# Two sets of buffers for the first layer norm, and the query rotation moved into the loop over head pairs

## The reference

```python
# x: (8, 4096, 1024) float32; _layernorm has no weights, eps 1e-5
x = x + attn_a(_layernorm(x))   # linear attention: elu(Q)+1, elu(K)+1, KV = K^T V, context = Q KV / Z, @ Wo.T + bo
x = x + ffn(_layernorm(x))      # gelu(x @ w1 + b1) @ w2 + b2, 1024 -> 4096 -> 1024
x = x + attn_b(_layernorm(x))   # below
x = x + ffn(_layernorm(x))

# attn_b: 16 heads of 64; causal softmax attention
q = (x @ Wq) split in heads
k = low-rank keys: x @ Wk (192 columns), expanded by key_decoder
v = low-rank values: x @ Wv (192 columns), expanded by value_decoder
q = _apply_rope(q, cos, sin)
k = _apply_rope(k, cos, sin)
attn = softmax(mask(q k^T / 8))
y = (attn v) @ Wproj
```

## Time and profile before

| | us |
|---|---|
| median of two runs of the kernel | 6642.1 (6566.71 and 6717.48) |
| the profiled execution, its own time | 6563.59 |
| its span on the slowest core (core 0) | 6562.1 |
| spans of the other cores | 6528.1 to 6555.6 |

### The profile page before, as it was taken

The page is one execution under the profiler, slowest core; times in us unless marked ns, Lnnn a source line. Parts: engine busy times, 40 slices in busy tenths (PEclk is TensorE's granted clock), DMA queues, the critical chain, the costliest instruction groups (busy, mean ns, idle before and its releaser), DMA issues.

```text
span 6562.1 us, 55992 instructions; the slowest of 8 cores (6528.1 to 6562.1 us)
## 1 busy us (share of the span) xinstructions
PE 4754.6 (72%) x19134; PEld 1766.6 (27%) x19408; DVE 1540.7 (23%) x2479; ACT 1823.9 (28%) x2415; POOL 81.6 (1%) x158
## 2 busy tenths in 40 slices
PE   2299767775996888572877777777785556996777
PEld 0033222222442333221222222222221112442333
DVE  3344354451001222127022022012102440000000
ACT  1110011102331000000755855765672002330000
POOL 0000000000001000000000000000000000001000
PEclk6599888887998888795877877977887777998888
DMA  2200211114226333200000000000003224226333
GB/s 65 64 1 1 39 52 52 39 39 101 76 76 146 103 103 103 63 0 0 6 5 5 6 6 5 6 6 5 5 6 97 84 91 96 75 76 146 109 103 115
DMA packets 258100, 356.21 MB, mean 54 GB/s; under 512 B 19173, under 2 KB 166885, under 8 KB 255526
## 3 DMA queue, kind: packets, MB, share of 16 engines
q1 hardware_dynamic: 236294, 304.50, 14.1%
q0 software_dynamic: 21536, 48.12, 4.2%
HBM read 257.93 MB, written 142.74 MB: 61 GB/s over the span
## 4 chain that ended last, share of the span: by engine, by line
PE 61%; DVE 12%; ACT 11%; DMA 8%; issue 5%; DVEq 2%; POOL 1%; ACTq 1%; SPq 0%; POOLq 0%
ACT expb L833 7%; PE f2pyo L569 7%; PE f1pyo L569 7%; PE f1pph L523 6%; PE f2pph L523 6%; PE py L797 4%; PE psc L814 4%; PE py L801 3%; PE pr L917 2%; PE ppt L475 2%; PE ppk L303 2%; PE ppb L457 2%; PE p L668 2%; PE pkv L341 2%; PE ppv L311 2%
## 5 line engine op out<-in xcount | busy, mean ns | idle before, releaser
L833 ACT ACTIVATE expb<-psc 128x1024 bf16<-128x1024 f32 x896 | 892.6, 1023 | 179.7 <-PE psc L821 167.5
L797 PE MATMUL py<-expb,vpair 128*65 128x512 bf16 (+3 forms) x1152 | 469.3, 407 | 297.5 <-ACT expb L833 275.3
L569 PE MATMUL f2pyo<-f2hb,f2w 128*128 128x512 bf16 x2007 | 467.2, 394 | 153.8 <-DMA f2hb<-scr_h 123.8
L523 PE MATMUL f1pph<-xnt,f1w 128*128 128x512 bf16 x2007 | 446.7, 381 | 63.6 <-DMA f1w<-w 57.4
L523 PE MATMUL f2pph<-xnt,f2w 128*128 128x512 bf16 x2007 | 445.8, 380 | 62.6 <-DMA f2w<-w 56.4
L569 PE MATMUL f1pyo<-f1hb,f1w 128*128 128x512 bf16 x2004 | 463.2, 392 | 37.8 <-DMA f1w<-w 29.1
L814 PE MATMUL psc<-xnt,kpair 64*128 64x512 bf16 (+3 forms) x1152 | 472.8, 410 | 6.5 <-DVE vpair L754 6.5
L821 PE MATMUL psc<-xnt,kpair 64*128 64x512 bf16 (+3 forms) x1152 | 472.8, 410 | 0.0
L801 PE MATMUL py<-expb,vpair 128*65 128x512 bf16 (+3 forms) x1152 | 469.3, 407 | 0.0
L776 DVE CAST ybuf<-py 64x512 bf16<-64x512 f32 x64 | 43.7, 683 | 1495.2 <-PE py L801 1464.7
L569 PEld LDWEIGHTS f2pyo<-f2hb,f2w 128*128 128x128 bf16 x2048 | 205.4, 101 | 415.5 <-issue 190.9
(11 more groups left out here) (192 smaller groups left out, 4818.4 us busy)
## 6 DMA issues: line engine op xcount, KB each, us to landing
p_xf<-xT SPq DMA_DIRECT2D x16, 2048.0 KB, 8.6
scr_h<-f1hs SPq DMA_DIRECT2D x256, 128.0 KB
f1hb<-scr_h SPq DMA_DIRECT2D x32, 1024.0 KB
scr_h<-f2hs SPq DMA_DIRECT2D x256, 128.0 KB
f2hb<-scr_h SPq DMA_DIRECT2D x32, 1024.0 KB
scr<-p_x1f SPq DMA_DIRECT2D x8, 2048.0 KB, 6.9
f1xf<-scr SPq DMA_DIRECT2D x8, 2048.0 KB, 15.5
scr<-f1x2f SPq DMA_DIRECT2D x8, 2048.0 KB, 8.1
```

The lines of the kernel that those rows point to most:

```text
L523: ins = T.matmul(pph[b][:, :], w1s[kt][:, jt * 128:jt * 128 + 128], self.xnt[kt][:, cols], start=(kt == 0), stop=(kt == NT - 1))
L569: ins = T.matmul(pyo[ot][:, :], w2s[jt][:, ot * 128:ot * 128 + 128], hb[g % 2][:, jj * 512:jj * 512 + 512], start=(jt == 0), stop=(jt == N ...
L797: T.matmul(py0[0:65, pcol0:512], vpair[:, pt * 130:pt * 130 + 65], expb[pbank][:, pcol0:512], start=(pt == 0), stop=(pt == plast))
L833: exp_free[bank] = ss.inc(Sc.activation(expb[bank][:, :], psc[bank][:, :], AF.Exp, scale=0.125))
```

## The change

In phase 0 the chunk tile, its bf16 and squared copies, the three statistics rows and the three kinds of PSUM tile exist twice, and chunks take turns in them. The load of chunk `ch` now waits for the layer norm of chunk `ch - 2`. The loads count on `sh[0]` and `sh[1]` in turn. The order of the instructions on every engine is unchanged.

In `attn_b` the separate loop that rotated all query tiles, and the barrier behind it, are gone. The same seven instructions stand in a function `rope_q(t)` with buffers `qA` and `qB` of its own. `rope_q(0)` is called ahead of the loop over head pairs, and `rope_q(p + 1)` at the head of pair `p`, ahead of the line that sets `prod_free`. TensorE waits for the rotation of its own pair before the scores.

```diff
-    def load_chunk_f32(self, dst, dram, c0, width=512):
+    def load_chunk_f32(self, dst, dram, c0, width=512, ctr=None):
         return self.lq_on(
-            self.sx,
+            self.sx if ctr is None else ctr,
...
-    def emit_ln(self, src, xb, xsq, dst_tiles, dc0, pstats, pbm, pbr):
+    def emit_ln(self, src, xb, xsq, dst_tiles, dc0, pstats, pbm, pbr, rows=None):
...
+        r_mean, r_var, r_rstd = rows if rows is not None else (
+            self.r_mean, self.r_var, self.r_rstd)
...
-            ln_done = 0
+            xf = [E(nc.sbuf_tensor(f"p0_xf{i}", [128, NT * 512], F32)) for i in range(2)]
...
+            ln_done = [0, 0]
             for ch in range(8):
+                b = ch % 2
                 c0 = ch * 512
-                self.w(Q, self.sv, ln_done)
-                e_x = self.load_chunk_f32(xf, self.dxT, c0)
-                self.w(V, self.sx, e_x)
-                self.w(Sc, self.sx, e_x)
-                ln_done = self.emit_ln(xf, xb, xsq, self.xnt, c0, pstats, pbm, pbr)
+                self.w(Q, self.sv, ln_done[b])
+                e_x = self.load_chunk_f32(xf[b], self.dxT, c0, ctr=self.sh[b])
+                self.w(V, self.sh[b], e_x)
+                self.w(Sc, self.sh[b], e_x)
+                ln_done[b] = self.emit_ln(xf[b], xb[b], xsq[b], self.xnt, c0,
+                                          pstats[b], pbm[b], pbr[b], rows=rows[b])
...
-                self.w(V, sq, sq.n)
-                for t in range(NT):
+                qA = E(nc.sbuf_tensor("qropeA", [128, S], BF16))
+                qB = E(nc.sbuf_tensor("qropeB", [128, S], BF16))
+
+                def rope_q(t):
+                    self.w(V, sq, sq.n)
                     V.drain()
...
-                    sv.inc(V.tensor_tensor(self.xnt[t][:, :], tA[:, :], tB[:, :], ALU.add))
-                self.barrier()
+                    return sv.inc(V.tensor_tensor(self.xnt[t][:, :], qA[:, :], qB[:, :],
+                                                  ALU.add))
...
+                rope_evt = [0] * (NT + 1)
+                rope_evt[0] = rope_q(0)
                 for p in range(8):
+                    if p + 1 < NT:
+                        rope_evt[p + 1] = rope_q(p + 1)
                     prod_free = [sv.n, sv.n]
...
                     self.w(T, sv, e_kpair)
+                    self.w(T, sv, rope_evt[p])
```

More of the change, by code:

```diff
@@ L205, in emit_ln @@
         self.w(V, st, e_stats)
-        V.tensor_single_scalar(self.r_mean[:, :], pstats[0:1, :], 1.0 / D, ALU.mult)
-        V.tensor_scalar(self.r_var[:, :], pstats[32:33, :], 1.0 / D, EPS,
+        V.tensor_single_scalar(r_mean[:, :], pstats[0:1, :], 1.0 / D, ALU.mult)
+        V.tensor_scalar(r_var[:, :], pstats[32:33, :], 1.0 / D, EPS,
                         op0=ALU.mult, op1=ALU.add)
         V.drain()
-        V.tensor_tensor(self.r_rstd[:, :], self.r_mean[:, :], self.r_mean[:, :], ALU.mult)
+        V.tensor_tensor(r_rstd[:, :], r_mean[:, :], r_mean[:, :], ALU.mult)
         V.drain()
-        e_rows = sv.inc(V.tensor_tensor(self.r_var[:, :], self.r_var[:, :],
-                                        self.r_rstd[:, :], ALU.subtract))
+        e_rows = sv.inc(V.tensor_tensor(r_var[:, :], r_var[:, :],
+                                        r_rstd[:, :], ALU.subtract))
         self.w(Sc, sv, e_rows)
-        Sc.activation(self.r_rstd[:, :], self.r_var[:, :], AF.Ln)
+        Sc.activation(r_rstd[:, :], r_var[:, :], AF.Ln)
         Sc.drain()
-        e_rstd = ss.inc(Sc.activation(self.r_rstd[:, :], self.r_rstd[:, :],
+        e_rstd = ss.inc(Sc.activation(r_rstd[:, :], r_rstd[:, :],
                                       AF.Exp, scale=-0.5))
@@ L220, in emit_ln @@
         self.w(T, ss, e_rstd)
-        T.matmul(pbm[:, :], self.ones_rf[:, :], self.r_mean[:, :], start=True, stop=True)
-        e_bc = st.inc(T.matmul(pbr[:, :], self.ones_rf[:, :], self.r_rstd[:, :],
+        T.matmul(pbm[:, :], self.ones_rf[:, :], r_mean[:, :], start=True, stop=True)
+        e_bc = st.inc(T.matmul(pbr[:, :], self.ones_rf[:, :], r_rstd[:, :],
                                start=True, stop=True))
@@ L237, in phase0 @@
             E = p.enter_context
[L238 to L243, removed]
-            ln_done = 0
+            xf = [E(nc.sbuf_tensor(f"p0_xf{i}", [128, NT * 512], F32)) for i in range(2)]
+            xb = [E(nc.sbuf_tensor(f"p0_xb{i}", [128, NT * 512], BF16)) for i in range(2)]
+            xsq = [E(nc.sbuf_tensor(f"p0_xsq{i}", [128, NT * 512], BF16)) for i in range(2)]
+            rows = [(E(nc.sbuf_tensor(f"p0_rm{i}", [1, 512], F32)),
+                     E(nc.sbuf_tensor(f"p0_rv{i}", [1, 512], F32)),
+                     E(nc.sbuf_tensor(f"p0_rs{i}", [1, 512], F32))) for i in range(2)]
+            pstats = [E(nc.psum_tensor(f"p0_pstats{i}", [33, 512], F32)) for i in range(2)]
+            pbm = [E(nc.psum_tensor(f"p0_pbm{i}", [128, 512], F32)) for i in range(2)]
+            pbr = [E(nc.psum_tensor(f"p0_pbr{i}", [128, 512], F32)) for i in range(2)]
+            ln_done = [0, 0]
             for ch in range(8):
+                b = ch % 2
                 c0 = ch * 512
-                self.w(Q, self.sv, ln_done)
-                e_x = self.load_chunk_f32(xf, self.dxT, c0)
-                self.w(V, self.sx, e_x)
-                self.w(Sc, self.sx, e_x)
-                ln_done = self.emit_ln(xf, xb, xsq, self.xnt, c0, pstats, pbm, pbr)
+                self.w(Q, self.sv, ln_done[b])
[4 more added lines that the diff above has]
+                                          pstats[b], pbm[b], pbr[b], rows=rows[b])
         self.barrier()
@@ L682, in attn_b @@
                 tB = E(nc.sbuf_tensor("ropeB", [128, S], BF16))
-                self.w(V, sq, sq.n)
-                for t in range(NT):
+                qA = E(nc.sbuf_tensor("qropeA", [128, S], BF16))
+                qB = E(nc.sbuf_tensor("qropeB", [128, S], BF16))
+                def rope_q(t):
+                    self.w(V, sq, sq.n)
                     V.drain()
[L686 to L689, removed]
+                    V.tensor_copy(qB[0:32, :], self.xnt[t][32:64, :])
+                    V.tensor_copy(qB[32:64, :], self.xnt[t][0:32, :])
+                    V.tensor_copy(qB[64:96, :], self.xnt[t][96:128, :])
+                    V.tensor_copy(qB[96:128, :], self.xnt[t][64:96, :])
                     V.drain()
-                    V.tensor_tensor(tA[:, :], self.xnt[t][:, :], cosr[:, :], ALU.mult)
-                    V.tensor_tensor(tB[:, :], tB[:, :], sinr[:, :], ALU.mult)
+                    V.tensor_tensor(qA[:, :], self.xnt[t][:, :], cosr[:, :], ALU.mult)
+                    V.tensor_tensor(qB[:, :], qB[:, :], sinr[:, :], ALU.mult)
                     V.drain()
-                    sv.inc(V.tensor_tensor(self.xnt[t][:, :], tA[:, :], tB[:, :], ALU.add))
-                self.barrier()
+                    return sv.inc(V.tensor_tensor(self.xnt[t][:, :], qA[:, :], qB[:, :],
+                                                  ALU.add))
                 kpre = tA
```

## The result

| | before | after |
|---|---|---|
| median of the runs, us | 6690.3 (10 runs) | 6634.3 (11 runs) |
| undisturbed runs, us | 6564.0 to 6567.0 | 6520.2 to 6525.0 |
| their ratio, with 95% interval | | 0.9935 [0.9918, 0.9952] |
| span of the slowest core in the profile, us | 6562.1 | 6542.4 |
| median over the eight cores of the profile, stage by stage, summed | 6544.3 | 6499.4 |

The kernel became 0.65% faster, 43 us, where 1.1% and 70 us were forecast.

A forecast was written before the change was run, and what follows sets the result against it. TensorE, busy for 72% of the span, was taken as the bound, with gains only where it stands still. 6563.6 - 71.7 (phase 0) + 1.5 (query rotation) = 6493.4 us, 1.1% less; range 6453 to 6575 us.

The forecast's parts named there:

- I take nothing: Start of phase 0: issuing two loads together delays the first by 0 us, out of at most 8.3 to 11.1.
- A long gap cost nothing: Head pairs of attn_b: pair 0, after 102.80 us of standstill, took 235.3 us between key rotations, against a mean of 235.6.
- the displacement of the median: Whole kernel: the median of two runs lay 78.5 us above the profiled execution, so a later median could be 6572 us.
- Phase 0, 71.7 us: Phase 0: 63.3 us of exposed loads and 9.1 for the square go, 0.7 of drains comes back, 71.7 us less.
- loads and drains: Between chunks of phase 0: seven exposed loads, 63.3 us, go; seven drains of 0.1 us bring back 0.7.
- the square: Chunks of phase 0: ScalarE squares the already loaded chunk early, so 7 x 1.3 = 9.1 us go.
- The rotations stay in the open: attn_b: each query rotation waits behind the last tail in VectorE's queue; 95.5 us exposed in place of 95.7.
- the rotations do hide: Rival, attn_b: VectorE does six rotations under the scores, 72 us more go, 6422 us; chance 0.05.
- The price of a boundary, 0.5 us beyond the rotation: Between head pairs in attn_b: key products start at the lower clock, 0.5 us at six boundaries, 3 us more.
- the clock rival: Rival, attn_b: longer gaps make TensorE's clock return later; 12 us per boundary uses up the gain, double gives 6636; chance 0.05.
- 1.5 us for attn_b: attn_b net: 3.0 us for the clock, less 1.3 for the barrier and 0.2 for the rotations, 1.5 us slower.
- Within 2%: Whole kernel: the measured time differs from the kernel before by no more than 2%; chance 0.87.

The follow-up runs named there:

- the rotation was filled: The changed kernel plus 60 matmuls that nothing reads at the heads of pairs 1 to 6: first to last key rotation 1720.6 us, changed kernel 1730.7.

## Why the prediction was right or wrong

**It named the right mechanisms and gave too much for their sum, and its range missed the median.** Three of its steps failed: "I take nothing" for the first load, "A long gap cost nothing" for the loop, and the displacement of the median that made the range's upper end. Point by point:

*Phase 0, 71.7 us.* Measured -66.4 in the stage's median, and 292.88 - 223.95 = 68.9 us on core 0, from whose rows the forecast was made. There its terms hold closely: the gaps between a chunk's last multiply and the next cast (loads and drains) gave 62.6 us for 62.6, the chunks themselves (the square) 8.7 for 9.1. The step that failed is the one on the first load: "I take nothing, since both are issued one behind the other from one queue". The first cast was 2.5 us late on core 0, 3 in the median of the cores, within the bound of 8.3 to 11.1 that the text had, and issuing the second load later gave 3.1 back. The other 2.5 us between 68.9 and 66.4 are differences between cores: the median core ended phase 0 1.9 us earlier than core 0 before, and ends it 0.6 us later now. The ring order that the Trainium skill, DMA: Bandwidth & Descriptors, section "Queues, rings and completion order", tells of did not keep the second load from slowing the first; the same passage goes on that a later descriptor may finish its write before an earlier one, so an undisturbed first load didn't follow from it. The clock in phase 0 was rightly left as it was: the statistics of line 204 take 547 ns on core 0, 559 before, and the granted clock is 0.56 in the mean, before 0.55. It is also what makes chunks take 25.2 and 26.1 us in turn: on core 4 the last four statistics matmuls of the chunk at 98.11 ran at a clock of 1.00 and took 1.04 us, those of the next at 0.50 and took 1.91.

*The rotations stay in the open.* Right. The trace after shows one rotation behind each tail and 14.5 us of standstill for 14 forecast, the moved rotation alone gave 1.0012, and the same seven instructions at another place in VectorE's order gave 98 us. The rival "the rotations do hide" had been given 6422 us. The kernel in which they do has 6421 to 6425, but by luck, as two errors cancel: it starts from 6522 instead of 6493, and gains 98 us instead of 72, since seven rotations hide in it and the loop's ten us go with them.

*The price of a boundary, 0.5 us beyond the rotation.* Right for the boundary itself: 148.4 - 73.7 - 6 x 11.94 = 3.1 us on core 0, for 3 us forecast, and the first key products at 0.60 us, with 0.39 when the rotation was filled, show that it is the clock. What failed is the step "A long gap cost nothing". The loop grew by another 7.1 us, all between key rotation and last tail. Key rotations were to be 247.5 us apart and are (1730.7 - 235.6) / 6 = 249.2. The term was 1.5 us for attn_b and measured +10.3 (-72.4 + 81.8 + 0.9). That is 1.2 us for each boundary; the clock rival had the direction of it, and would have needed 12 to end slower than before. The step rested on the clock's first return in pairs 0 and 1, but the clock doesn't come back once. In pair 1 of the kernel before, core 0, it was up and down again within 15 us:

```profile
3387.00:3392.00 5.00, 4.54 (x21) 1.49 (x19) 0.00 (x0) 3.82 (x6) 0.00 (x0) 1.00 0.00 0
...
3397.00:3402.00 5.00, 3.35 (x9) 0.77 (x10) 0.00 (x0) 3.51 (x5) 0.00 (x0) 0.51 0.12 27
```

In pair 1 of the changed kernel the first return is even earlier, 61 us after the key rotation in place of 64, and the pair spends 4 us more at 1.2 GHz all the same. The sum of these times is what counts, 407 us against 385. Whether the longer gap causes it stays open, since the kernel with only the rotation moved has the same gaps and 388 us on core 0, 400 on core 4.

*What the sum left out.* In the first pair of profiles some 10 us more stand in the FFNs, without an instruction of the change in them. In the second half of the first FFN six undisturbed profiles with the new phase 0 (the changed kernel twice, and four of the experiments' kernels) had 688.6 to 691.3 us, the three without it 685.3, 686.3 and 687.3; TensorE waited there for DMA for 31.0 us in the mean of the cores before and 33.0 after. But a second pair of profiles, of both kernels on another occasion, gives another sum:

| after minus before, stage medians, us | forecast | first profiles | second profiles |
|---|---|---|---|
| phase 0 | -71.7 | -66.4 | -70.2 |
| attn_b, whole | +1.5 | +10.3 | +8.5 |
| attn_a | 0 | +1.2 | +3.2 |
| both FFNs | 0 | +10.1 | +2.0 |
| all | -70.2 | -44.9 | -56.5 |

(The undisturbed times of that occasion, 6516.8 us after and 6569.1 to 6573.4 before, differ by 52 to 57 us, where the first ones differ by 43.) So the kernel before alone varies by 4 us in phase 0 and 5 to 6 in the FFNs from one profile to the next, and of the 25 us that were missing at first only what attn_b has, 7 to 9 us beyond the forecast, stands in both. In phase 0 the cores used to end 7 us apart (289.4 to 296.0 at POOL's first weight load) and now end within 3 (223.7 to 226.7). That cores more in step ask for their weights at the same moments would explain a rise in the FFNs; it was only argued, since no kernel here moved the cores apart on purpose.

*The range.* Its upper end, 6575, came from "a median formed like that one would lie as much higher", a displacement of 78.5 us read from two runs. Over 11 runs the median lay 114 us above the lowest one, 6520.2, and the forecast for undisturbed runs, 6493, had the measured 6520 to 6525 outside its own narrow range of 6485 to 6502 too. Two runs 151 us apart don't say where the median of many will lie; its place between them was a guess. "Within 2%" was right.

## What to carry to other kernels

An instruction moved so that it can overlap has to stand, in the order of its own in-order engine, ahead of a wait that is long: here 12 us behind the last tail cost 12 to 14 us, and the same 12 us behind the fifth tail, with 29 us to go until the next one, cost none. The same holds for double buffers: they took 66 us out of phase 0, most of it waiting for loads, and the rest of the overlap, 53 us more, came only when the next chunk's first steps were written ahead of this chunk's last. The idle time shown in front of a waiting instruction is where the work should go; what stands behind that instruction can't use it.

## What the runs showed of the hardware that was not expected

- Two loads of 2048 KB issued one behind the other from one queue, on all eight cores at once, delay the first: the first cast came at 17.3 us in the median of the cores, at 14.35 with one load alone and at 14.3 when the second load was issued after the first had landed.
- The attention stretches repeat to 0.1 us from one execution to the next and over most cores (1582.3 us in both profiles of the changed kernel), yet differ by up to 9 us between kernels whose instructions in them are the same, and by up to 4.5 us between cores of one execution. The difference goes with the time that TensorE spends at 1.2 GHz in their scores, 372 to 411 us in seven pairs; what fixes that time stays open.
- Holding TensorE at 2.4 GHz up to the first scores (PEclk 1.00 from 3190 to 3210 us) didn't keep it there: it fell to 0.57 and 0.50 in the next two stretches of 10 us, with TensorE busy for 84 to 85% of each.
